# Two-layer cross-attention: layer-0 scores ahead of the value projection, and the later preparation spread over the first four units

## The chip, the cores and the metric

The kernel runs on one core of a Trainium2 chip. The metric is the device time of one execution in microseconds (us). TensorE (PE in the profile) multiplies matrices, VectorE is DVE, ScalarE is ACT, GpSimd is POOL, and SyncE is SP, which here only issues transfers. Each engine works through its own instructions in the order in which they are written, and semaphores hold an engine back until another engine or a transfer has got far enough.

## The reference

Two cross-attention layers over the same short context. x is 2 x 2048 x 512, the context is 2 x 77 x 512, the mask lets all or none of the 77 keys of a query through.

```python
# layer 0: one head of width 512
q = x @ Wq.T + bq;  k = ctx @ Wk.T + bk;  v = ctx @ Wv.T + bv
s = where(mask == 0, -1e9, q @ k.T)
x1 = softmax(s) @ v + x
# layer 1: 16 heads of width 32, then an output projection and a layer norm
Q, K, V = x1 @ Wq1.T + bq1, ctx @ Wk1.T + bk1, ctx @ Wv1.T + bv1
c = softmax(Q_h @ K_h.T / sqrt(32)) @ V_h        # for each head h
y = c @ Wo.T + bo + x1
out = layernorm(y) * gamma + beta
```

## The kernel before

The 4096 rows of x are cut into 8 blocks of 512 rows, which alternate between the two batches, and each block into 4 units; a unit is 4 heads of layer 1 (128 channels). Unit k belongs to block k // 4 and g = k % 4. Every engine runs `step(i, k)` for k = 0 to 33, which interleaves unit k with what is left of unit k - 1, the query of unit k + 1, the output projection and norm of the block before, and layer 0 of the block behind. The order inside a step is written out by hand.

Layer 0 is folded: the keys are multiplied into the query weights (`a0`, `c0`), so that scores come straight from x (`layer0`), and for each batch b the values are multiplied into layer 1's query weights (`fold`, whose product is `u`). Layer 1's query is then 14 matmuls (`query(i, k, first, last)`): 8 of x with the high and low half of the weights, 4 of x's low half, and 2 of the layer-0 probabilities with `u`. In those last two, matmuls 12 and 13, three parts of `u` are stacked on the 128 partitions: SP moves them from SBUF to SBUF with three transfers (`stack_weights`, which calls `move`, L262), and the third of these waits until VectorE has made the rest (`u_rest`). The same is done with the layer-0 probabilities of each block (`stack_probs`) and with the layer-0 value rows (`v0_a`, `v0_b`), which the output projection uses from step 5 on.

Ahead of step 0 stand the projections of the context (`project`, 32 recorded matmuls for a whole one): the keys k0T, the folded keys a0, the layer-0 values v0T, then `layer0(0, 0)`, layer 1's keys k1T, the transposes of v0T to rows (`to_rows`), `transpose0`, `fold(0)`, the first query, and between its parts layer 1's values v1T. Step 0 holds the transposes of v1T, step 1 the second fold, with `round_u(1)` on ScalarE and `u_rest(1)` on VectorE. On TensorE the wait for the second stacked `u` stands at the head of step 3, ahead of its scores:

```python
if type(i) is int and k == CH - 1:
    pe.wait_ge(u_stacked[1], 48)
...
scores(i, k)
```

Of the kernel before, what the change touches and what calls it, by code (L numbers as in the profile page):

```python
# [5 lines left out]
F32 = mybir.dt.float32  # L6
# [37 lines left out]
def xattn_kernel(nc, xT, x, mask, ctxT, w0k, w0q, w0v, w1q, w1k, w1v, w1o, cols, rows, out):  # L44
# [7 lines left out]
    with ExitStack() as ctx:  # L52
# [7 lines left out]
        with ExitStack() as prep:  # L60
            raw1 = sb("raw1", [P, CH, DIM], F32, prep)
            raw3 = sb("raw3", [P, CH, DIM], F32, prep)
            ctxT_sb = sb("ctxT_sb", [P, CH, BATCH * KEYS], F32, prep)
            v1T = sb("v1T", [P, CH, BATCH * KEYS], F32, prep)
            rest = sb("rest", [KEYS, BATCH, DIM], F32R, prep)
            v0T = sb("v0T", [P, CH, BATCH * KEYS], F32, prep)
            v0o = sb("v0o", [KEYS, BATCH, DIM], F32, prep)
            k0T = sb("k0T", [P, CH, BATCH * KEYS], F32, prep)
            raw0 = sb("raw0", [P, CH, DIM], F32, prep)
            bq0_wide = sb("bq0_wide", [P, CH, P], F32, prep)  # L70
            bo_sb = sb("bo_sb", [P, DIM], F32, prep)
            before_y = 4 * CH * BLOCK + KC * BLOCK + 2 * TILES * GCOLS
            taken = 3 * CH * DIM + 2 * BATCH * DIM + 4 * CH * BATCH * KEYS + CH * P + DIM
            sb("unused", [P, before_y - taken], F32, prep)
            raw2 = sb("raw2", [P, CH, DIM], F32, prep)
# [7 lines left out]

        wq_h = sb("wq_h", [P, CH, DIM], F32R)
# [132 lines left out]
        def _(sp):  # L217
# [5 lines left out]
            sp.dma_start(x_raw[:].rearrange("p c t -> p (c t)"), xT[0, 0]).then_inc(ld_xT, 16)  # L223
            sp.dma_start(raw3[:], w0v.rearrange("(c p) e -> p c e", p=P)).then_inc(ld_w0v, 16)
# [60 lines left out]
            stack_weights(v0_a, v0_b, slice(0, BATCH), v0_stacked, v0_h_ready, v0_ready, BATCH)  # L285

# [119 lines left out]
        def _(act):  # L406
            act.dma_start(cols_sb[:].rearrange("p a c -> p (a c)"), cols).then_inc(ld_cols, 16)
            act.dma_start(mask_sb[:].rearrange("p t k -> p (t k)"), mask[0, 0]).then_inc(ld_mask, 16)
            flat = rows.rearrange("(o n) -> o n", o=1)
            act.dma_start(bo_sb[:], flat[:, 2 * DIM:3 * DIM].to_broadcast([P, DIM])).then_inc(ld_bo, 16)  # L410
            act.dma_start(rows_sb[:].rearrange("p a d -> p (a d)"),
                          flat[:, 0:2 * DIM].to_broadcast([P, 2 * DIM])).then_inc(ld_rows, 16)
# [37 lines left out]
            leave(bank[1:3], mm_k0T, k0T, cols_sb[:, 1], k0T_ready)  # L450
            round_x(0, 0, 0, CH)
            leave(bank[5:7], mm_v0T, v0T, cols_sb[:, 2], v0T_ready)
            exp0(0, 0)
# [3 lines left out]
            act.wait_ge(bk1_ready, 1)  # L457
            leave(bank[1:3], mm_k1T, k1T, bk1_scaled, k1T_ready, scale=SCALE)
# [5 lines left out]

            round_u(0)
            leave(bank[5:7], mm_v1T, v1T, cols_sb[:, 5], v1T_ready, first=0, last=2)
            round_q(0, 0)
            leave(bank[5:7], mm_v1T, v1T, cols_sb[:, 5], v1T_ready, first=2, last=CH)
# [31 lines left out]
            def step(i, k):  # L500
                g, b = k % CH, k // CH
                round_ct(i, k - 2)
                leave_pt(i, k - 1, 0)
                exps(i, k, 0)
                if type(i) is int and k == 0:
                    for v in range(BATCH):
                        act.wait_ge(mm_v1, v + 1)
                        nc.scalar.activation(v1[:, v], bank[5 + v][0:KEYS, :], ACT.Copy).then_inc(v1_ready, 1)
                if g == 3:
                    round_p0(i, b + 1)  # L510
                leave_pt(i, k - 1, 1)
                exps(i, k, 1)
                if g == 1:
                    exps(i, k, 2)
                    round_x(i, b + 1, 0, 1)
                    exps(i, k, 3)
                    leave_pt(i, k - 1, 2)
                    round_x(i, b + 1, 1, 2)
                    leave_pt(i, k - 1, 3)
                    exp0(i, b + 1)  # L520
                else:
                    leave_pt(i, k - 1, 2)
                    exps(i, k, 2)
                    if g == 2:
# [16 lines left out]
                if type(i) is int and k == 0:  # L541
                    act.wait_ge(ld_w1o, 16)
                    for c in range(CH):
                        nc.scalar.activation(wo_h[:, c], raw3[:, c], ACT.Copy).then_inc(wo_h_ready, 1)
# [7 lines left out]
        def _(dve):  # L552
# [68 lines left out]
            dve.wait_ge(c0_ready, 1)  # L621
            layer0_leave(0, 0)
# [4 lines left out]
            for c in range(CH):  # L627
                dve.wait_ge(wq_h_ready, c + 1)
                nc.vector.tensor_tensor(wq_l[:, c], raw2[:, c], f32(wq_h[:, c]), ALU.subtract).then_inc(wq_ready, 1)
            def u_rest(b):  # L630
                dve.wait_ge(u_h_ready, b + 1)
                if b == 1:
                    dve.wait_ge(v0_stacked, 48)
                nc.vector.tensor_tensor(rest[:, b], bank[5 + 2 * b][0:KEYS, :], f32(u_a[0:KEYS, b]), ALU.subtract).then_inc(u_ready, 1)
# [3 lines left out]
            dve.wait_ge(ld_bo, 16)  # L638
            for b in range(BATCH):
                dve.wait_ge(mm_v0, b + 1)  # L640
                nc.vector.tensor_tensor(v0o[:, b], bank[3 + b][0:KEYS, :], bo_sb[0:KEYS], ALU.add).then_inc(v0o_ready, 1)
            for v in range(BATCH):
                dve.wait_ge(v0o_ready, v + 1)
                nc.vector.tensor_copy(v0_a[0:KEYS, v], v0o[:, v]).then_inc(v0_h_ready, 1)
            for v in range(BATCH):
                dve.wait_ge(v0_h_ready, v + 1)
                dve.wait_ge(u_stacked[0], 48)
# [73 lines left out]
            def step(i, k):  # L721
# [72 lines left out]
        def _(pe):  # L794
# [12 lines left out]
            def to_rows(banks, src, made):  # L807

                for b in range(BATCH):
                    for e in range(CH):  # L810
                        mm = nc.tensor.transpose(banks[b][0:KEYS, e * P:(e + 1) * P],
                                                 src[:, e, b * KEYS:(b + 1) * KEYS], ident[:])
                    mm.then_inc(made, 1)
# [142 lines left out]
            project(bank[5:7], raw3, ctxT_sb, mm_v0T, [ld_w0v, ld_w0v])  # L956
# [16 lines left out]

            transpose0(0, 0)
            fold(0, 0, CH)
            pe.wait_ge(wq_ready, CH)
            query(0, 0, 0, 3 * CH)
            pe.wait_ge(u_ready, 1)
            pe.wait_ge(p0l_ready, 1)
            project(bank[5:7], raw1, ctxT_sb, mm_v1T, [ld_w1v, ld_w1v], 0, 2)  # L980
            pe.wait_ge(u_stacked[0], 48)
            query(0, 0, 3 * CH, QUERY)
            project(bank[5:7], raw1, ctxT_sb, mm_v1T, [ld_w1v, ld_w1v], 2, CH)
            pe.wait_ge(k1T_ready, CH)
            pe.wait_ge(v0o_ready, BATCH)

            def step(i, k):
# [13 lines left out]
                if type(i) is int and k == 0:  # L1001
                    pe.wait_ge(v1T_ready, CH)
                    to_rows(bank[5:7], v1T, mm_v1)
                if type(i) is int and k == 1:
                    pe.wait_ge(v1_ready, BATCH)
# [10 lines left out]
                if type(i) is int and k == 1:  # L1016
                    pe.wait_ge(add0_done, 2)
                    fold(1, 0, 2)
                if g == 0:
# [13 lines left out]
                if type(i) is int and k == 1:  # L1033
                    fold(1, 2, CH)
                if g == 0:
# [48 lines left out]
```

## Time and profile before

| | us |
|---|---|
| median of 3 runs | 436.24 |
| lowest and highest run | 433.89, 436.6 |
| the profiled execution: its own time | 433.85 |
| its span, first to last instruction | 432.1 |
| TensorE busy | 395.1 (91%) |
| ScalarE, VectorE, GpSimd busy | 281.4, 273.3, 222.0 |

How to read it: the profile's page gives each engine's busy share in 40 slices of the span, and the chain of waits that ended last. The timeline gives groups of instructions in order of time, with the idle time before a group and what ended it. A row of windows gives busy time of each engine in one stretch, with the granted clock of TensorE in it (1.00 is 2.4 GHz, 0.50 is 1.2 GHz). The rows that the prediction uses stand in a section below.

### The profile page before, as it was taken

What the parts mean: (1) busy time and instruction counts of PE and PEld (TensorE: products, weight loads), DVE (VectorE), ACT (ScalarE), POOL (GpSimd) and SP (SyncE); (2) the same over time, 40 slices, a digit from 0 to 9 for tenths busy, and PEclk for the clock granted to TensorE, in tenths of its full rate; (3) what the DMA queues carried; (4) which work ended last, traced back from release to release, by engine and by line L of the source; (5) the groups of instructions that cost most, each with busy time, mean ns of one, the idle gap of its engine ahead of it and who ended that gap; (6) DMA issues with size and microseconds to landing.
All of it is one profiled execution on the core that took longest, in us unless ns stands there. A gap on an engine that the chain in (4) does not pass through costs nothing.

```text
span 432.1 us, 12183 instructions
## 1 busy us (share of the span) xinstructions
PE 395.1 (91%) x4968; PEld 298.2 (69%) x4968; DVE 273.3 (63%) x679; ACT 281.4 (65%) x813; POOL 222.0 (51%) x245
## 2 busy tenths in 40 slices
PE   4999997799999999999999999999999998997960
PEld 4996755577767687777777776767776776775840
DVE  0145466467766875786668776677677866476256
ACT  0432777676688676876588558856785778667122
POOL 0400366225547843784378547755576537534353
PEclk9999999999999999999999999999999999999895
DMA  8993103400042302330053005320413012600112
GB/s 263 400 324 101 41 4 126 139 6 3 2 141 77 123 2 85 133 124 2 26 189 104 24 2 168 102 72 2 165 68 110 0 31 76 215 5 9 42 49 97
DMA packets 19230, 39.44 MB, mean 91 GB/s; under 512 B 1865, under 2 KB 5449, under 8 KB 18151
## 3 DMA queue, kind: packets, MB, share of 16 engines
q1 hardware_dynamic: 18599, 37.72, 25.8%
q10 hardware_dynamic: 576, 0.96, 0.7%
q8 instruction: 39, 0.64, 0.7%
q14 instruction: 16, 0.13, 0.1%
HBM read 26.49 MB, written 8.39 MB: 81 GB/s over the span
## 4 chain that ended last, share of the span: by engine, by line
PE 75%; DVE 12%; ACT 5%; DMA 4%; issue 1%; SPq 1%; POOL 0%; DVEq 0%
PE ps_q L864 19%; PE ps_out L929 17%; PE ps_t L889 11%; PE ps_s L878 7%; PE ps_pv L904 7%; PE ps_out L825 4%; PE ps_s L801 4%; PE ps_s L944 2%; ACT prob L475 2%; DVE mx L655 2%; DMA p_b<-p_l 2%; DVE m L573 2%; DVE sm L662 1%; ACT pt L484 1%; DMA raw<-in_w0k 1%
## 5 line engine op out<-in xcount | busy, mean ns | idle before, releaser
L339 POOL TENSOR_TENSOR prob<-prob,rc 128x308 f32<-128x308 f32 x128 | 91.9, 725 | 158.8 <-DVE rc L664 157.6
L475 ACT ACTIVATE prob<-ps_s,mx 128x77 f32<-128x77 f32 x512 | 121.2, 328 | 0.7 <-DVE mx L655 0.7
L484 ACT ACTIVATE pt<-ps_t 77x512 f32<-77x512 f32 x128 | 76.3, 596 | 57.6 <-PE ps_t L889 57.0
L655 DVE TENSOR_REDUCE mx<-ps_s 128x4 f32<-128x308 f32 x128 | 54.8, 471 | 46.8 <-PE ps_s L878 46.8
L889 PE MATMUL ps_t<-ident,prob 128*77 128x128 f32 x512 | 79.8, 279 | 3.9 <-ACT pt L484 3.3
L662 DVE TENSOR_REDUCE sm<-prob 128x4 f32<-128x308 f32 x128 | 59.6, 466 | 35.0 <-ACT prob L475 34.9
L889 PEld LDWEIGHTS ps_t<-ident,prob 128*77 128x77 f32 x512 | 61.8, 148 | 23.7 <-issue 8.7
L864 PE MATMUL ps_q<-x_h,wq_h 128*128 128x512 f32 x128 | 53.4, 417 | 0.0
L864 PE MATMUL ps_q<-x_h,wq_l 128*128 128x512 f32 x128 | 53.0, 414 | 0.0
L318 POOL TENSOR_TENSOR x_l<-x_raw,x_h 128x512 fp32r<-128x512 f32 x32 | 41.2, 1292 | 21.2 <-ACT x_h L428 21.2
L929 PE MATMUL ps_out<-wo_h,ct_h 128*128 128x512 f32 x112 | 46.3, 413 | 0.0
L878 PEld LDWEIGHTS ps_s<-k1T,q 32*64 32x64 f32 x2048 | 25.8, 130 | 28.6 <-issue 15.5
L929 PE MATMUL ps_out<-wo_l,ct_h 128*128 128x512 f32 x112 | 44.3, 395 | 0.0
L929 PE MATMUL ps_out<-wo_h,ct_l 128*128 128x512 f32 x112 | 44.1, 394 | 0.0
L355 POOL TENSOR_TENSOR y<-y,rows_sb 128x512 f32<-128x512 f32 x28 | 36.0, 1286 | 13.6 <-ACT y L497 13.6
L864 PE MATMUL ps_q<-x_l,wq_h 128*128 128x512 f32 x128 | 41.0, 404 | 0.0
L357 POOL TENSOR_TENSOR y<-y,rows_sb 128x512 f32<-128x512 f32 x28 | 36.1, 1288 | 2.2
L904 PE MATMUL ps_pv<-pt,v 77*32 77x512 f32 x256 | 34.1, 602 | 1.6 <-ACT pt L484 1.6
L490 ACT ACTIVATE ct_h<-ps_pv 128x512 fp32r<-128x512 f32 x32 | 19.2, 600 | 24.8 <-PE ps_pv L904 24.7
L446 ACT ACTIVATE q<-ps_q,cols_sb 128x512 f32<-128x512 f32 x32 | 22.2, 694 | 18.2 <-PE ps_q L864 18.1
L878 PE MATMUL ps_s<-k1T,q 32*64 32x77 f32 x2048 | 31.1, 238 | 2.7 <-ACT q L446 1.8
L670 DVE TENSOR_TENSOR ct_l<-ps_pv,ct_h 128x512 fp32r<-128x512 f32 x32 | 21.8, 680 | 9.8 <-ACT ct_h L490 9.8
(111 smaller groups left out, 608.5 us busy)
## 6 DMA issues: line engine op xcount, KB each, us to landing
x_raw<-in_xT SPq DMA_DIRECT2D x8, 1024.0 KB, 6.5
y<-in_x SPq DMA_DIRECT2D x28, 256.0 KB, 2.8
out<-y SPq DMA_DIRECT2D x28, 256.0 KB, 2.0
p_b<-p_a SPq DMA_DIRECT2D x8, 154.0 KB
mask_sb<-in_mask SPq DMA_DIRECT2D x7, 154.0 KB, 5.4
raw<-in_w0k SPq DMA_DIRECT2D x2, 512.0 KB, 6.8
raw<-in_w0q SPq DMA_DIRECT2D x2, 512.0 KB, 10.0
raw<-in_w0v SPq DMA_DIRECT2D x1, 1024.0 KB, 12.2
```

The costliest lines, as they stand in the source:

```text
L318: nc.gpsimd.tensor_tensor(x_l[:, b % 2, c], x_raw[:, c], f32(x_h[:, b % 2, c]), ALU.subtract).then_inc(xl_ready, 1)
L339: nc.gpsimd.tensor_tensor(ap, ap, wide(rc[:, k % 2, h], KEYS), ALU.mult).then_inc(prob_done, 1)
L357: nc.gpsimd.tensor_tensor(y[:, t], y[:, t], rows_sb[:, 1], ALU.add).then_inc(beta_done, 1)
L475: e = nc.scalar.activation(prob[:, k % 2, h, t], ps_s[:, h, t * KEYS:(t + 1) * KEYS], ACT.Exp, bias=mx[:, k % 2, h, t:t + 1])
L484: nc.scalar.activation(pt[:, h], ps_t[0:KEYS, :], ACT.Copy).then_inc(pt_ready, 1)
L655: nc.vector.reduce_max(mx[:, k % 2, h], ps_s[:, h, 0:TILES * KEYS].rearrange("p (t k) -> p t k", k=KEYS), AX_X, negate=True).then_inc(max_ ...
L662: nc.vector.reduce_sum(sm[:, k % 2, h], prob[:, k % 2, h], AX_X).then_inc(sum_done, 1)
L864: mm = nc.tensor.matmul(ps_q[:], w, v, start=(m == 0), stop=(m == QUERY - 1))
L878: mm = nc.tensor.matmul(ps_s[r:r + P // 2, h, t * KEYS:(t + 1) * KEYS], q[rows_of, k % 2, t * P + r:t * P + r + P // 2], k1T[rows_of, g, b ...
L889: mm = nc.tensor.transpose(ps_t[0:KEYS, t * P:(t + 1) * P], prob[:, k % 2, h, t], ident[:])
L904: mm = nc.tensor.matmul(ps_pv[rows_of, :], v1[:, b % 2, own], pt[:, h], start=True, stop=True)
L929: mm = nc.tensor.matmul(ps_out[:], w, v, start=(m == 0), stop=(m == OUTPUT - 1))
```

## The change

- TensorE: `layer0(0, 0)` comes right behind the folded keys, ahead of v0T. Six matmuls of the first query come ahead of `transpose0` and `fold(0)`, the other six of its first twelve behind. k1T comes behind these. v1T moves into step 0, behind the scores, and its transposes to the end of step 0. `fold(1)` moves from step 1 to step 2. The transposes of v0T move into step 3, one batch in the middle and one near the end, and use the bank `ps_out`.
- ScalarE and VectorE follow this order: `round_u(1)` and `u_rest(1)` move to step 2, the value rows (`v0_leave`, `v0_rest`) to step 3 on VectorE; the low half of the query weights (`wq_rest`) is made around the first layer-0 softmax.
- Transfers: the first mask goes from ScalarE's queue to SP's, behind x. The two loads of bo, gamma and beta are issued by ScalarE behind its copies of k0T and not at its start. On SP the stacking of the value rows goes behind that of the second block's probabilities, and `next_inputs(0, 1)` goes ahead of these.
- `rest` and `bo_sb` get memory of their own. The wait at the head of step 3 is as it was.

```diff
@@ SP
             sp.dma_start(x_raw[:].rearrange("p c t -> p (c t)"), xT[0, 0]).then_inc(ld_xT, 16)
+            sp.dma_start(mask_sb[:].rearrange("p t k -> p (t k)"), mask[0, 0]).then_inc(ld_mask, 16)
             sp.dma_start(raw3[:], w0v.rearrange("(c p) e -> p c e", p=P)).then_inc(ld_w0v, 16)
...
             stack_weights(u_a, u_b, slice(0, 1), u_stacked[0], u_h_ready, u_ready, 1)
-            stack_weights(v0_a, v0_b, slice(0, BATCH), v0_stacked, v0_h_ready, v0_ready, BATCH)
-
             stack_weights(u_a, u_b, slice(1, 2), u_stacked[1], u_h_ready, u_ready, 2)
             sp.wait_ge(mm_u, BATCH)
             sp.wait_ge(wq_ready, CH)
             for t in range(TILES):
                 load_rows(0, 0, t)
+            next_inputs(0, 1)
             stack_probs(0, 1)
-            next_inputs(0, 1)
+            stack_weights(v0_a, v0_b, slice(0, BATCH), v0_stacked, v0_h_ready, v0_ready, BATCH)
@@ ScalarE
-            leave(bank[5:7], mm_v0T, v0T, cols_sb[:, 2], v0T_ready)
-            exp0(0, 0)
             act.wait_ge(ld_w1q, 16)
             for c in range(CH):
                 nc.scalar.activation(wq_h[:, c], raw2[:, c], ACT.Copy).then_inc(wq_h_ready, 1)
-            act.wait_ge(bk1_ready, 1)
-            leave(bank[1:3], mm_k1T, k1T, bk1_scaled, k1T_ready, scale=SCALE)
+            leave(bank[5:7], mm_v0T, v0T, cols_sb[:, 2], v0T_ready, first=0, last=2)
+            exp0(0, 0)
+            leave(bank[5:7], mm_v0T, v0T, cols_sb[:, 2], v0T_ready, first=2, last=CH)
             round_p0(0, 0)
...
-                if type(i) is int and k == 1:
+                if k == 0:
+                    round_wo(0, 3)
+                if k == 2:
                     round_u(1)
                 round_q(i, k + 1)
@@ VectorE
+            wq_rest(0)
+            wq_rest(1)
             layer0_leave(0, 0)
             layer0_mask(0, 0)
             layer0_select(0, 0)
             layer0_shift(0, 0)
+            wq_rest(2)
             layer0_probs(0, 0)
+            wq_rest(3)
...
+                if k == 3:
+                    v0_leave(0)
                 inverse_sums(i, k, 3)
-                if type(i) is int and k == 1:
+                if k == 2:
                     u_rest(1)
+                if k == 3:
+                    v0_leave(1)
+                    v0_rest(0)
+                    v0_rest(1)
@@ TensorE
-            project(bank[5:7], raw3, ctxT_sb, mm_v0T, [ld_w0v, ld_w0v])
             pe.wait_ge(a0_ready, 2)
             pe.wait_ge(c0_ready, 1)
             layer0(0, 0)
-            project(bank[1:3], raw0, ctxT_sb, mm_k1T, [ld_w1k, ld_w1k])
-            pe.wait_ge(v0T_ready, CH)
-            pe.wait_ge(ident_ready, 1)
-            to_rows(bank[3:5], v0T, mm_v0)
-            pe.wait_ge(ld_w1q, 16)
+            project(bank[5:7], raw3, ctxT_sb, mm_v0T, [ld_w0v, ld_w0v])
...
+            pe.wait_ge(wq_ready, 3)
+            query(0, 0, 0, 6)
+            pe.wait_ge(ident_ready, 1)
+            pe.wait_ge(v0T_ready, CH)
             transpose0(0, 0)
             fold(0, 0, CH)
             pe.wait_ge(wq_ready, CH)
...
```

TensorE ahead of the first unit, before (a is the folded keys, raw a weight matrix as loaded, m the layer-0 probabilities):

```order
L801 MATMUL ps_s<-k0T,raw 128x154 x16
L954 MATMUL ps_out<-k0T,bq_wide 128x154 x4
L801 MATMUL ps_t<-ctxT_sb,raw 128x154 x8
L801 MATMUL ps_pv<-ctxT_sb,raw 128x154 x8
L825 MATMUL ps_out<-a,x_raw 32x77 x64
L801 MATMUL ps_s<-ctxT_sb,raw 128x154 x16
L811 MATMUL ps_s<-ident,v0T 77x128 x8
L838 MATMUL ps_pv<-ident,m 77x128 x4
L969 MATMUL ps_t<-raw,v0T 77x512 x4
```

The same place in the change (L840 waits for a0 and c0, which VectorE copies out; the first L879 for three of the four pieces of the weights' low half; L853 for the layer-0 probabilities and v0T):

```order
L969 MATMUL ps_out<-k0T,bq_wide 128x154 x4
L840 MATMUL ps_out<-a,x_raw 32x77 x64
L818 MATMUL ps_t<-ctxT_sb,raw 128x154 x8
L818 MATMUL ps_pv<-ctxT_sb,raw 128x154 x8
L879 MATMUL ps_q<-x_h,wq_h 128x512
L879 MATMUL ps_q<-x_h,wq_l 128x512
...
L853 MATMUL ps_pv<-ident,m 77x128 x4
L979 MATMUL ps_t<-raw,v0T 77x512 x4
```

The layer-0 scores (L840) now follow the folded keys without the v0T projection between them, and the start of the first query (six matmuls of L879, of which the first is shown) stands behind v0T and ahead of the transposes.

TensorE from the end of step 2 to the transposes of step 3, in the change (L893 are the scores of step 3, which wait for q, for the exponentials of step 2 and for the second stacked `u`):

```order
L979 MATMUL ps_out<-raw,v0T 77x512 x2
L879 MATMUL ps_q<-x_l,wq_h 128x512 x2
L879 MATMUL ps_q<-p_a,u_a 128x512
L879 MATMUL ps_q<-p_b,u_b 128x512
L919 MATMUL ps_pv<-pt,v 32x512 x4
L893 MATMUL ps_s<-k1T,q 64x77 x32
L904 MATMUL ps_t<-ident,prob 77x128 x4
L853 MATMUL ps_pv<-ident,m 77x128 x4
```

The second half of the second fold (L979) now stands in the same step as, and some eight matmuls ahead of, the scores that wait for its stacked copy; before, a whole step lay between them.

SP in the change, from the second stacked `u` on (its first row waits for `round_u(1)`, its third for `u_rest(1)`):

```order
L263 DMA u_a<-u_a 51x512
L263 DMA u_b<-u_a 26x512
L263 DMA u_b<-rest 77x512
L248 DMA y<-in_x 128x512 x4
L241 DMA x_raw<-in_xT 128x2048
L242 DMA mask_sb<-in_mask 128x308
L263 DMA p_b<-p_a 77x512
L263 DMA p_a<-p_l 51x512
L263 DMA p_b<-p_l 26x512
L263 DMA v_a<-v_a 51x1024
```

Before, the x_raw and mask loads stood behind the three p moves, and the v moves ahead of the second u moves.

## Rows read from the trace of the kernel before

**Rows 1.** The page: busy shares and granted clock in 40 slices.
```profile
PE   4999997799999999999999999999999998997960
PEclk9999999999999999999999999999999999999895
```

**Rows 2.** Windows: us, busy us (count) by engine, granted clock, DMA share, GB/s.
```profile
51.59:64.46 12.87, 10.98 (x119) 6.42 (x121) 7.58 (x21) 9.45 (x28) 8.21 (x9) 1.00 0.01 2
64.46:73.47 9.01, 7.32 (x103) 5.12 (x103) 5.88 (x15) 7.94 (x25) 6.14 (x7) 1.00 0.49 153
73.47:84.56 11.09, 8.20 (x114) 5.54 (x117) 5.43 (x14) 7.41 (x23) 4.34 (x6) 1.00 0.39 114
200.00:400.00 200.00, 193.58 (x2409) 143.21 (x2408) 140.02 (x357) 146.54 (x430) 117.88 (x130) 1.00 0.23 75
```

**Rows 3.** Chain of waits ahead of step 2: start us, us, what held it.
```profile
1.24 5.00 DMA raw<-in_w0k
6.37 7.35 PE ps_s L801 x32
14.46 4.47 PE ps_s L801 x32
24.18 2.27 PE ps_out L825 x128
30.86 0.87 PE ps_s L811 x8
32.17 3.45 PE ps_t L969 x8
42.03 2.10 PE ps_pv L801 x16
46.04 3.27 PE ps_q L864 x14
```

**Rows 4.** Windows of the start: to the first matmul, and to 12.3 us.
```profile
0.00:6.20 6.20, 0.00 (x0) 0.00 (x0) 0.51 (x2) 0.00 (x0) 0.75 (x7) 1.00 0.70 193
6.37:12.30 5.93, 5.93 (x23) 5.93 (x24) 0.00 (x0) 1.39 (x2) 0.00 (x0) 1.00 1.05 371
```

**Rows 5.** Transfers: issues, KB each, us from issue to landing.
```profile
raw<-in_w1q SPq DMA_DIRECT2D x1, 1024.0 KB, 13.7
```

**Rows 6.** Timeline of SP: start us, us to issue.
```profile
7.33 2.19 SPq L225 DMA_DIRECT2D raw<-in_w1q  x1
```

**Rows 7.** Timeline of ScalarE and VectorE ahead of step 0.
```profile
29.83 2.17 ACT L456 ACTIVATE wq_h<-raw 128x512 fp32r<-128x512 f32 x4
20.02 0.32 DVE L620 COPY c<-ps_out 128x154 f32<-128x154 f32 x1 [0.57 <-PE ps_out L954]
26.60 0.48 DVE L560 TENSOR_TENSOR m<-ps_out,c 128x308 f32<-128x308 f32 x1 [6.26 <-PE ps_out L825]
28.95 0.48 DVE L592 TENSOR_TENSOR m<-m,stat 128x308 f32<-128x308 f32 x1
31.07 2.49 DVE L629 TENSOR_TENSOR wq_l<-raw,wq_h 128x512 fp32r<-128x512 f32 x4
42.07 0.69 ACT L446 ACTIVATE q<-ps_q,cols_sb 128x512 f32<-128x512 f32 x1 [0.86 <-PE ps_q L864]
```

**Rows 8.** Chain: from the first u to its stacked copy, and the probabilities' last move.
```profile
35.64 0.60 ACT u_a L463
37.83 3.42 DMA u_b<-rest
78.97 3.82 DMA p_b<-p_l
```

**Rows 9.** Timeline of TensorE: two waits, in brackets the idle time and its releaser.
```profile
41.30 0.50 PE L864 MATMUL ps_q<-p_a,u_a 128*128 128x512 f32 x1 [0.80 <-DMA u_b<-rest]
73.47 0.94 PE L878 MATMUL ps_s<-k1T,q 32*64 32x77 f32 x64 [0.83 <-ACT q L446]
```

**Rows 10.** Windows: the stretch ahead of a half clock, and the half clock.
```profile
398.00:401.40 3.40, 1.67 (x9) 1.25 (x8) 3.26 (x8) 0.86 (x2) 3.32 (x5) 1.00 0.21 80
401.40:404.80 3.40, 3.40 (x12) 2.75 (x11) 1.26 (x2) 0.24 (x1) 1.79 (x2) 0.50 0.20 77
```

More of the change, by code:

```diff
@@ L81, in xattn_kernel @@
         y = sb("y", [P, TILES, DIM])
+        rest = sb("rest", [KEYS, BATCH, DIM], F32R)
+        bo_sb = sb("bo_sb", [P, DIM])
         wq_h = sb("wq_h", [P, CH, DIM], F32R)
@@ L450, in _ @@
             leave(bank[1:3], mm_k0T, k0T, cols_sb[:, 1], k0T_ready)
+            flat = rows.rearrange("(o n) -> o n", o=1)
+            act.dma_start(bo_sb[:], flat[:, 2 * DIM:3 * DIM].to_broadcast([P, DIM])).then_inc(ld_bo, 16)
+            act.dma_start(rows_sb[:].rearrange("p a d -> p (a d)"),
+                          flat[:, 0:2 * DIM].to_broadcast([P, 2 * DIM])).then_inc(ld_rows, 16)
             round_x(0, 0, 0, CH)
-            leave(bank[5:7], mm_v0T, v0T, cols_sb[:, 2], v0T_ready)
-            exp0(0, 0)
             act.wait_ge(ld_w1q, 16)
@@ L463, in round_u, with round_wo @@
                 nc.scalar.activation(u_a[0:KEYS, b], bank[5 + 2 * b][0:KEYS, :], ACT.Copy).then_inc(u_h_ready, 1)
+            def round_wo(first, last):
+                act.wait_ge(ld_w1o, 16)
+                for c in range(first, last):
+                    nc.scalar.activation(wo_h[:, c], raw3[:, c], ACT.Copy).then_inc(wo_h_ready, 1)
             round_u(0)
-            leave(bank[5:7], mm_v1T, v1T, cols_sb[:, 5], v1T_ready, first=0, last=2)
+            act.wait_ge(bk1_ready, 1)
+            leave(bank[1:3], mm_k1T, k1T, bk1_scaled, k1T_ready, scale=SCALE)
             round_q(0, 0)
-            leave(bank[5:7], mm_v1T, v1T, cols_sb[:, 5], v1T_ready, first=2, last=CH)
             def exps(i, k, h):
@@ L504, in step @@
                 exps(i, k, 0)
[L505 to L508, printed above, removed]
                 if g == 3:
@@ L521, in step @@
                 else:
+                    if k == 0:
+                        leave(bank[5:7], mm_v1T, v1T, cols_sb[:, 5], v1T_ready, first=0, last=2)
                     leave_pt(i, k - 1, 2)
                     exps(i, k, 2)
+                    if k == 0:
+                        leave(bank[5:7], mm_v1T, v1T, cols_sb[:, 5], v1T_ready, first=2, last=CH)
                     if g == 2:
@@ L540, in step @@
                     normalise(i, b - 2, 3)
[L541 to L544, printed above, removed]
+                if k == 0:
+                    for v in range(BATCH):
+                        act.wait_ge(mm_v1, v + 1)
+                        nc.scalar.activation(v1[:, v], bank[5 + v][0:KEYS, :], ACT.Copy).then_inc(v1_ready, 1)
+                    round_wo(3, CH)
             run(act, step)
@@ L621, in _, with wq_rest @@
             dve.wait_ge(c0_ready, 1)
+            def wq_rest(c):
+                dve.wait_ge(wq_h_ready, c + 1)
+                nc.vector.tensor_tensor(wq_l[:, c], raw2[:, c], f32(wq_h[:, c]), ALU.subtract).then_inc(wq_ready, 1)
+            wq_rest(0)
+            wq_rest(1)
             layer0_leave(0, 0)
@@ L637, in _, with v0_leave, v0_rest @@
             u_rest(0)
[L638 to L642, printed above, removed]
+            def v0_leave(v):
+                dve.wait_ge(ld_bo, 16)
+                dve.wait_ge(mm_v0, v + 1)
+                nc.vector.tensor_tensor(v0o[:, v], ps_out[0:KEYS, :], bo_sb[0:KEYS], ALU.add).then_inc(v0o_ready, 1)
                 dve.wait_ge(v0o_ready, v + 1)
                 nc.vector.tensor_copy(v0_a[0:KEYS, v], v0o[:, v]).then_inc(v0_h_ready, 1)
-            for v in range(BATCH):
+            def v0_rest(v):
                 dve.wait_ge(v0_h_ready, v + 1)
-                dve.wait_ge(u_stacked[0], 48)
+                dve.wait_ge(u_stacked[v], 48)
                 nc.vector.tensor_tensor(rest[:, v], v0o[:, v], f32(v0_a[0:KEYS, v]), ALU.subtract).then_inc(v0_ready, 1)
@@ L805, in project, with to_rows @@
                         mm.then_inc(made, 1)
[L807 to L813, printed above, removed]
+            def to_rows(to, src, b, made):
+                for e in range(CH):
+                    mm = nc.tensor.transpose(to[0:KEYS, e * P:(e + 1) * P], src[:, e, b * KEYS:(b + 1) * KEYS], ident[:])
+                mm.then_inc(made, 1)
             def layer0(i, b):
@@ L976, in _ @@
             pe.wait_ge(wq_ready, CH)
[L977 to L980, printed above, removed]
+            query(0, 0, 6, 3 * CH)
+            project(bank[1:3], raw0, ctxT_sb, mm_k1T, [ld_w1k, ld_w1k])
             pe.wait_ge(u_stacked[0], 48)
             query(0, 0, 3 * CH, QUERY)
-            project(bank[5:7], raw1, ctxT_sb, mm_v1T, [ld_w1v, ld_w1v], 2, CH)
             pe.wait_ge(k1T_ready, CH)
-            pe.wait_ge(v0o_ready, BATCH)
             def step(i, k):
@@ L1000, in step @@
                 scores(i, k)
[L1001 to L1004, printed above, removed]
+                if k == 0:
+                    pe.wait_ge(u_ready, 1)
+                    pe.wait_ge(p0l_ready, 1)
+                    project(bank[5:7], raw1, ctxT_sb, mm_v1T, [ld_w1v, ld_w1v])
+                if k == 1:
                     pe.wait_ge(v1_ready, BATCH)
@@ L1015, in step @@
                     last_output(0, 3, [1])
-                if type(i) is int and k == 1:
+                if k == 2:
                     pe.wait_ge(add0_done, 2)
                     fold(1, 0, 2)
+                if k == 3:
+                    pe.wait_ge(u_ready, 2)
+                    to_rows(ps_out, v0T, 0, mm_v0)
                 if g == 0:
@@ L1032, in step @@
                 transposes(i, k - 1, 3)
-                if type(i) is int and k == 1:
+                if k == 0:
+                    pe.wait_ge(v1T_ready, CH)
+                    for v in range(BATCH):
+                        to_rows(bank[5 + v], v1T, v, mm_v1)
+                if k == 2:
                     fold(1, 2, CH)
+                if k == 3:
+                    pe.wait_ge(v0o_ready, 1)
+                    to_rows(ps_out, v0T, 1, mm_v0)
                 if g == 0:
```

19 lines of the change are left out of this document (4 added, 15 removed).

## The prediction

> **What bounds the kernel now.** I read the page first. TensorE is busy in nearly every slice, and its granted clock is full until close to the end [rows 1]. The reader is to see that the matrix work sets the time: of the 200 us in the middle it fills 193.58 [rows 2]. The change leaves out no matmul and adds none; it only puts them in another order, all of it ahead of step 4. So it can win only idle time of TensorE in the first 85 us, and whatever it wins or loses there is kept to the end, since the steps behind have hardly any slack to give back.
>
> Then I took windows of the steps. Step 1 lasts 12.87 us with 10.98 busy, step 2 9.01 with 7.32, step 3 11.09 with 8.20 [rows 2]: 1.9, 1.7 and 2.9 us idle. Ahead of step 0 TensorE waits 5.00 us for the first half of w0k, and 0.80 us for the stacked u [rows 3, 9]. That, 6.5 us in the steps, and the 0.76 us from the end of the first projection (6.37 + 7.35 us) to 14.46 is all that there is to win [rows 3]. Last I read the timelines and the chain for the lengths of single pieces.
>
> **The start.** Until 6.2 us the transfers moved 193 GB/s times 6.2 us, 1.2 MB [rows 4]. The first matmul needs the context (0.32 MB by its size) and half of w0k (0.52 MB). The other 0.36 MB are mask, bo, gamma and beta, which ScalarE's queue issued alongside; at the 371 GB/s of the next stretch they are worth 1.0 us. They now go later. I take **-1.0 us**; between nothing (the queue of SP is no faster alone) and -1.4. The first matmuls run slowly: 23 in 5.93 us until 12.3 us, then 11 of the same kind in the 1.4 us that are left, about the two levels of the clock, although the column says 1.00 for the first stretch [rows 3, 4]. I let that slow stretch keep its length.
>
> **From there to step 0**, on a clock that starts 1.0 us earlier. The folded keys a0 run from 13.4 to 17.9 (4.47 us), c0 to 18.9. Layer-0 scores now come at once, and must wait for VectorE's copy of c0, which before started at 20.02, 0.04 after its matmul, and took 0.32 [rows 7]: a new wait of 0.4 us, which v0T covered before. Scores end at 21.6 (2.27), v0T at 25.8 (twice 2.10) [rows 3]. The first query needs three pieces of the low half of the weights. w1q landed at 7.33 + 13.7 = 21.0 us [rows 5, 6], and I leave it there, since the same bytes stand ahead of it. ScalarE rounds a piece in 0.54 (2.17 for four), so two are there at 22.1, and VectorE's two subtractions (0.62 each) end at 22.9. Only then does VectorE start on the layer-0 scores, which lay ready at 21.6. Its chain to the shifted scores took from 26.60 to 29.43 [rows 7], 2.8 us; it ends at 25.8 and the third piece at 26.4. TensorE waits 0.6 us. Six query matmuls (3.27 us for 14) give 27.8, transposes 28.3, fold 31.8 (3.45), six more 33.2, k1T 37.6. The first u took from 35.64 to 37.83 + 3.42 = 41.25 to be stacked [rows 8], 5.6 us; from 31.8 that is 37.4, just hidden by k1T. With k1T gone from there it would be 4.2 us of waiting, so this cover is thin. Two matmuls and ScalarE's 0.69 us for q then lie open [rows 7], 0.8 us, because v1T no longer stands over them: step 0 starts at 39.2. New waits 0.4 + 0.6 + 0.8, one of 0.8 gone: **+1.0 us**, between 0 (w1q lands earlier, since less competes with it early) and +2 (the stacked u behind the loads of w1o and x, which SP now issues later).
>
> **Step 0** takes in v1T and its transposes. ScalarE's copies of it stand between exponentials and are done before the query ends. Cover: v1T's 4.2 us and the query's 3.3; without it each copy (0.7 us for two) would show. Nothing.
>
> **Step 1** loses the fold (3.45). Its two halves stood over ScalarE's exponentials and copies of the transposes, so part of what goes comes back as idle time: I take 2.6 us instead of 1.9, **+0.7**, between 0 and +1.7 (half of the fold).
>
> **Step 2** gains the fold, and there it fills the 1.7 us of idle time whole: 7.32 + 3.45 = 10.8 us without a gap. **-1.7**, at the least -1.2. The wait for q at the end of it, 0.83 us [rows 9], is part of that.
>
> **Step 3: the wait that was free.** The scores of step 3 stand behind the wait for the second stacked u, which only matmuls 12 and 13 of the next query need. Before, u came out of step 1 and was in place long ahead. Now the fold ends some eight matmuls (4 of the query, 4 of the context, 0.23 us each, 1.9 us) before TensorE gets to these scores: 8.9 us into a step of 10.8. ScalarE takes u behind its last exponentials and a rounding of x, at about 9.1, and 5.6 us later it is stacked, at 14.7. TensorE stands still from 10.8 on: **+4.0 us**. Behind that wait are queued the scores, with them VectorE's maxima, ScalarE's exponentials, GpSimd's scaling, and the layer-0 transposes; nothing runs meanwhile that TensorE will need less of. At the least 3.0 (u taken at once, a shorter landing), at the most 5.0 (ScalarE half a us late, y's loads in the way). The row has 3.42 us from issue to landing of the last part. The Trainium skill, "DMA: Bandwidth & Descriptors", section "Anatomy of one DMA — SWDGE (gpsimd) path", gives a fixed 2.0 us plus the bytes at 436 GB/s, so 2.4 us for this one: by that the wait is 3.0 and the sum 1.0 smaller; the row is of this very transfer, and decides.
>
> **The rest of step 3.** The value rows' transposes (0.87 us in all [rows 3]) come in. The first half fills a wait for the copies; the second must wait until VectorE has taken the first out of `ps_out`, an operation as long as a wq_l (0.62), and delays the last query matmuls by some 0.5 us. Work +0.9, length +0.6: **-0.3**, between -0.6 and +0.3. SP moves p behind the loads of y and x now, 2 MB, but these are issued at the end of the wait and the p moves 5 us later: hidden; if they were not, half a us. Removing v0's moves from ahead of u's costs nothing, SP stood idle.
>
> **The clock.** After a stretch with 1.67 busy of 3.40 us TensorE got half clock for 3.40 us, near the end [rows 10]. In the wait of 4.0 us it does nothing at all. I expect the same there: 3.4 us at half clock are worth up to 1.7 us, but half of step 3's start waits for other engines: **+0.8**, between 0 and 1.7.
>
> Sum: -1.0 + 1.0 + 0.7 - 1.7 + 4.0 - 0.3 + 0.8 = **+3.5 us**. Against the profiled execution's own 433.85 us (its span of 432.1 and 1.75 around it) that is 437.35. That execution was at the low end of the runs; against their median of 436.24 it is 439.7, and that is my number.
>
> **Rivals.**
> 1. *Slower than 1%.* The clock stays at half for a second such stretch, so that the wait costs 3.4 us of clock and not 0.8: +6.1, 442.3. For it: no stretch in [rows 10] is as idle as this wait. Against: the half clock there lasted one stretch although TensorE was only just back at work. It decides once more than 1.7 us are lost. The change not doing at the start what it says (w0k no earlier, +4.5, 440.7) leads near it too. Together 0.30.
> 2. *The clock is kinder.* No half clock at the wait (-0.8), the slow first stretch shorter (5.93 us at half clock cost 3.0; half as long, -1.5), the one near the end missing (-1.7): 3.5 - 4.0 = -0.5, 435.7. For it: all three hang on where the clock changes. Against: the end of the program is untouched. 0.14. The Trainium skill, "TensorE: Matmul & The Clock Gate", section "What's actually happening", says that activity releases the throttle and idleness brings it back, and that the point of change shifts from run to run: it bears on both cases.
> 3. *Faster than 1%.* The stacked u is in place before the scores of step 3, so the wait costs nothing, and the clock is as in 2: -4.5, 431.7. It would need 5.6 us of stacking in 1.7. 0.06.
>
> The forecast itself, 437.3 to 440.6, has 0.50. The bounds of the terms, taken as independent, give 2.3 us to either side of the sum, 437.4 to 442.0; with case 2 and the second stretch of case 1 the range is 435.5 to 442.5. About 1% (4.4 us) can be told from no change. Faster by over that: 0.06; slower: 0.30; between: 0.64.
>
> **What would show it.** Right: TensorE idle for about 4 us ahead of the scores of step 3, released by the transfer of u's rest; the first matmul near 5.3 us; step 0 starting near 39, step 3 near 75 and step 4 near 87 where it was 84.56; step 2 without gaps; a 0.50 in the clock at 75. Wrong: a wait under 3 us or none there; step 0 later than 41 (the front then lost what it won); step 1 shorter than 9.5. The total is wrong if steps 4 to 33 differ in length between the two, where I expect none.

## The result, and the profile after

| | before | after |
|---|---|---|
| median (4 runs each) | 435.06 | 444.81 |
| lowest and highest | 433.89, 436.6 | 439.73, 448.04 |
| profiled execution, own time | 433.85 | 439.73 |
| its span | 432.1 | 437.9 |

The ratio is 1.0197, 95% interval 1.014 to 1.0253: slower, by 1.4 to 2.5%. Run again on another occasion the changed kernel took 443.36 us against 433.91 (ratio 1.0191, 1.0134 to 1.0248). The ratios leave out every execution more than 1.5% above the fastest of its kernel, such as the 448.04 here, while the medians count all. The sum for the profiled execution, 437.35, missed its 439.73 by 2.4 us, and it is the fastest of the four; the median lies 5 us above it.

The page after. TensorE's busy time is the same 395.1 us; the clock row has its dent at slice 8, where before there was none [rows 1]:

```profile
PE   4888977889999999999999999999999998999860
PEclk9999999699999999999999999999999999999995
```

The wait that was forecast, in the timeline of TensorE after (start us, us, work, and in brackets the idle time before it and its releaser). Step 3's scores start at 77.89, 4.14 us after TensorE had reached them:

```profile
63.20 0.95 PE L893 MATMUL ps_s<-k1T,q 32*64 32x77 f32 x64
...
72.68 1.06 PE L919 MATMUL ps_pv<-pt,v 77*32 77x512 f32 x8
...
77.89 1.42 PE L893 MATMUL ps_s<-k1T,q 32*64 32x77 f32 x64 [4.14 <-DMA u_b<-rest]
...
88.99 0.66 PE L827 MATMUL ps_out<-ident,v0T 128*77 128x128 f32 x4 [1.25 <-DVE v0o L652]
...
91.51 1.01 PE L893 MATMUL ps_s<-k1T,q 32*64 32x77 f32 x64
```

Windows after: steps 1, 2 and 3 (to compare with [rows 2]), then the wait and what follows it (start and end, us, then busy us and in brackets the count of instructions for PE, PEld, DVE, ACT and POOL, then the granted clock, the DMA share and GB/s):

```profile
52.27:63.20 10.93, 7.62 (x108) 5.09 (x103) 7.34 (x21) 7.72 (x24) 5.39 (x6) 1.00 0.00 1
63.20:73.75 10.55, 10.54 (x114) 6.35 (x110) 5.85 (x15) 8.42 (x25) 8.45 (x10) 1.00 0.01 2
77.89:91.51 13.62, 11.45 (x114) 8.39 (x114) 7.85 (x19) 7.01 (x22) 2.80 (x4) 0.76 0.50 178
73.75:77.40 3.65, 0.00 (x0) 0.00 (x0) 0.00 (x0) 0.60 (x1) 0.79 (x1) 1.00 0.41 107
77.50:84.30 6.80, 5.83 (x79) 4.76 (x80) 3.48 (x8) 2.03 (x6) 0.22 (x1) 0.50 0.89 326
```

Step 2 has no gap, as forecast. In the wait TensorE is busy for 0.00 us, and from 77.5, shortly before it ends, the clock is at 0.50 for 6.8 us, twice as long as in [rows 10].

And the front, timeline of TensorE: behind the first wait for w0k five gaps up to the scores of step 0, 3.7 us together, where before there was one of 0.80, beside the 0.76 for k0T that both kernels have [rows 9] (two of the five have no releaser in the profile, marked issue; the first of them, 0.46, stands where the wait for c0 was forecast):

```profile
5.53 6.23 PE L818 MATMUL ps_s<-ctxT_sb,raw 128*128 128x154 f32 x32 [5.53 <-DMA raw<-in_w0k]
...
18.50 2.35 PE L840 MATMUL ps_out<-a,x_raw 128*32 128x77 f32 x128 [0.46 <-issue]
...
24.55 1.58 PE L818 MATMUL ps_pv<-ctxT_sb,raw 128*128 128x154 f32 x10 [0.62 <-issue]
...
26.81 0.50 PE L879 MATMUL ps_q<-x_h,wq_h 128*128 128x512 f32 x1 [0.68 <-DVE wq_l L630]
...
38.99 0.50 PE L879 MATMUL ps_q<-p_a,u_a 128*128 128x512 f32 x1 [1.05 <-DMA u_b<-rest]
...
40.59 0.94 PE L893 MATMUL ps_s<-k1T,q 32*64 32x77 f32 x64 [0.87 <-ACT q L441]
```

### The profile page after: what moved, and what is told of

Read it like the earlier page. It is cut to its first block, busy times and chain, and to the rows that moved or that the text cites. A ratio compares the mean times of both kernels' runs of the same rounds, so it can differ in the third digit from the quotient of the medians.

```text
span 437.9 us, 12183 instructions
## 1 busy us (share of the span) xinstructions
PE 395.1 (90%) x4968; PEld 297.9 (68%) x4968; DVE 272.0 (62%) x679; ACT 281.3 (64%) x813; POOL 221.7 (51%) x245
## 4 chain that ended last, share of the span: by engine, by line
PE 72%; DVE 12%; DMA 6%; ACT 5%; SPq 2%; issue 2%; POOL 0%; DVEq 0%
PE ps_q L879 20%; PE ps_out L944 17%; PE ps_t L904 11%; PE ps_s L893 7%; PE ps_pv L919 6%; PE ps_out L840 4%; DMA raw<-in_w1q 3%; ACT prob L478 2%; PE ps_s L959 2%; DMA u_b<-rest 2%; DVE mx L666 2%; ACT pt L487 2%; DVE m L579 1%; DVE sm L673 1%; PE ps_pv L853 1%
## 5 line engine op out<-in xcount | busy, mean ns | idle before, releaser
L879 PE MATMUL ps_q<-x_h,wq_h 128*128 128x512 f32 x128 | 54.4, 425 | 0.7 <-DVE wq_l L630 0.7
L879 PE MATMUL ps_q<-x_h,wq_l 128*128 128x512 f32 x128 | 53.6, 419 | 0.0
L893 PEld LDWEIGHTS ps_s<-k1T,q 32*64 32x64 f32 x2048 | 26.1, 133 | 32.2 <-issue 15.1
L355 POOL TENSOR_TENSOR y<-y,rows_sb 128x512 f32<-128x512 f32 x28 | 36.0, 1286 | 12.1 <-ACT y L500 12.1
L879 PE MATMUL ps_q<-x_l,wq_h 128*128 128x512 f32 x128 | 41.0, 404 | 0.0
L893 PE MATMUL ps_s<-k1T,q 32*64 32x77 f32 x2048 | 31.3, 241 | 6.3 <-DMA u_b<-rest 4.1
L493 ACT ACTIVATE ct_h<-ps_pv 128x512 fp32r<-128x512 f32 x32 | 19.1, 598 | 26.2 <-PE ps_pv L919 26.2
L879 PEld LDWEIGHTS ps_q<-x_h,wq_h 128*128 128x128 f32 x128 | 24.7, 193 | 4.1 <-DVE wq_l L630 0.9
```

Source lines behind the costliest of these rows:

```text
L355: nc.gpsimd.tensor_tensor(y[:, t], y[:, t], rows_sb[:, 0], ALU.mult).then_inc(gamma_done, 1)
L879: mm = nc.tensor.matmul(ps_q[:], w, v, start=(m == 0), stop=(m == QUERY - 1))
L893: mm = nc.tensor.matmul(ps_s[r:r + P // 2, h, t * KEYS:(t + 1) * KEYS], q[rows_of, k % 2, t * P + r:t * P + r + P // 2], k1T[rows_of, g, b ...
```

## The experiments

Ratios are to the kernel before in runs on the same chips, with their 95% intervals.

| kernel | median us | ratio |
|---|---|---|
| changed, again | 443.36 | 1.0191 (1.0134 to 1.0248) |
| changed, late wait | 446.48 | 1.0274 (1.023 to 1.0318) |
| before + second fold in step 2 | 439.01 | 1.0116 (1.0074 to 1.0157) |
| changed, wait filled | 440.60 | 1.0146 (1.0098 to 1.0195) |
| changed, p ahead of loads | 444.80 | 1.0220 (1.0163 to 1.0278) |
| both of these | 439.03 | 1.0069 (1.0032 to 1.0107) |
| and the first u ahead of loads | 433.69 | 0.9987 (0.9955 to 1.0019) |
| and VectorE's order | 433.91 | 0.9976 (0.994 to 1.0012) |
| before + the loads alone | 433.97 | 0.9981 (0.9958 to 1.0005) |
| changed, fold back in step 1 | 438.27 | 1.0086 (1.0056 to 1.0116) |
| VectorE's order + split fold | 436.32 | 1.0050 (1.002 to 1.008) |
| and the second rows late | 434.31 | 0.9989 (0.9961 to 1.0016) |

**The changed kernel again.** 

> The changed kernel once more, unaltered, for the spread of its runs and a second profile. Theory W (the wait ahead of the scores of step 3 and the half clock that follows it): the wait is again 4.0 to 4.3 us, and only the length of the half clock behind it differs from execution to execution; the median is 441 to 446, over 5 us above before. Rival F (the new order ahead of step 0 is what varies): the wait is the same and step 0 starts later than 41 us in a slower execution.

Its profiled execution (442.02 us) waited 3.93 us ahead of step 3 and was at half clock from 77.8 to 84.6 us, much as the first; it started step 4 within 0.1 us of it. It took 2.2 us longer behind step 4 and shows one more half-clock stretch near the end. Theory W had the wait to within 0.1 us and the median right, but what differed between these two was the end, not the half clock behind the wait, and step 0 started at 41.0 at the latest (40.59 and 40.97).

**The wait moved to its reader.**

```diff
-                if type(i) is int and k == CH - 1:
-                    pe.wait_ge(u_stacked[1], 48)
...
                             wait(pe, p0_stacked, 48 * (blocks(i, b) + 1))
+                            if b == 1:
+                                pe.wait_ge(u_stacked[1], 48)
```

> The changed kernel with the wait for the second stacked u put right ahead of the two query matmuls that read it. Theory W: no idle time ahead of the scores of step 3, no half clock near 77 us, so 4.1 us of wait and all of the clock loss are gone; but the probabilities' moves now stand behind the loads of y and x on the same queue and land 1 to 2 us late: median 434 to 436.5, about as before. Rival F (front): 440 or more, since the front is untouched. Rival V (the value rows inside step 3 cost more than thought): 438 to 440.

A miss of 10 us: 446.48, slower than the changed kernel. The wait ahead of step 3 is gone, and in its place stand two others. Timeline of SP, and the chain of waits (start us, us):

```profile
79.98 1.86 SPq L248 DMA_DIRECT2D y<-in_x  x4
81.94 0.38 SPq L241 DMA_DIRECT2D x_raw<-in_xT  x1
...
84.46 0.80 SPq L263 DMA_DIRECT2D p_b<-p_l  x1
```

```profile
34.60 5.86 DMA u_b<-rest
...
84.46 7.57 DMA p_b<-p_l
```

The last probability move landed 7.57 us after its issue, with 2 MB of y and x issued 2.1 to 4.5 us ahead of it; in [rows 8] it took 3.82. TensorE waited 3.50 us for it and fell to half clock from 89.3 to 99.6. And the first u, behind the loads of w1o and x, landed after 5.86 us: TensorE waited 2.53, and was at half clock from 41.5 to 48.4. The first of these two the wait at step 3 had hidden: in the changed kernel's trace p's moves are issued 4.8 to 6.4 us behind the load of x. The second is not from this edit: the code is the changed kernel's up to there.

**One part alone: the second fold in step 2, in the kernel before.**

```diff
-                if type(i) is int and k == 1:
+                if type(i) is int and k == 2:
                     pe.wait_ge(add0_done, 2)
                     fold(1, 0, 2)
```

(and the same for its second half, `round_u(1)` and `u_rest(1)`)

> The kernel before, with one part of the change alone: the second fold, its rounding and its rest in step 2 and not in step 1, the wait at the head of step 3 as it was. Theory W: step 1 shorter by about 2.7 us, step 2 longer by about 1.7, then 4 us of wait and a half clock behind it: 439 to 446, slower than before by 4 us or more. Rival F: within 1 us of before, 434 to 436.5.

Theory W holds: 439.01, ratio 1.0116. Its timeline has the wait, as long as in the changed kernel, and half clock from 75.9 to 82.7. Step 1 became shorter by 1.2 us only, not by 2.7 (from 12.87 to 11.64):

```profile
77.09 1.42 PE L878 MATMUL ps_s<-k1T,q 32*64 32x77 f32 x64 [4.21 <-DMA u_b<-rest]
```

**The same delay without the idleness.**

```diff
                 if type(i) is int and k == CH - 1:
+                    for m in range(17):
+                        nc.tensor.matmul(ps_t[:], wq_h[:, m % CH, 0:P], x_h[:, 0, m % CH], start=True, stop=True)
                     pe.wait_ge(u_stacked[1], 48)
```

> The changed kernel with 17 extra matmuls of 512 columns ahead of the wait at the head of step 3 (they write a free bank, nobody reads the result), so that TensorE works for the 4.0 us in which it stood still. The delay is the same, only the idleness is gone. Theory W with the clock as the larger half: no half clock behind the wait, 437 to 439, and runs within 1 us of each other. Rival (the clock costs little, the loss beyond the wait is elsewhere): 442 to 446 as the changed kernel, with its spread.

440.60: between the two ranges. The clock did what the theory said, the time and its spread did not. In its profiled execution step 3 starts at 77.68, as late as in the changed kernel, but at full clock, and takes 11.60 us, not 13.62:

```profile
77.68:89.28 11.60, 8.97 (x116) 6.42 (x115) 7.84 (x19) 7.03 (x22) 2.80 (x4) 1.00 0.58 195
```

So the half clock there costs 2.0 us, beside 4.1 of plain waiting. The runs still spread over 7 us, so something else varies from execution to execution.

**The probability moves ahead of the loads, the wait as it was; then both.**

```diff
+            stack_probs(0, 1)
+            next_inputs(0, 1)
             sp.wait_ge(mm_u, BATCH)
             sp.wait_ge(wq_ready, CH)
             for t in range(TILES):
                 load_rows(0, 0, t)
-            next_inputs(0, 1)
-            stack_probs(0, 1)
```

> The changed kernel with the second block's probability moves put ahead of the loads of y and x on SP, the wait at the head of step 3 left as it was. If the wait hides the queue's order (theory W2), nothing moves: 4.1 us of wait, half clock behind it, 441 to 446. Rival (the order on the queue costs on its own, also in the changed kernel): 2 to 4 us less than the changed kernel, 438 to 441.

> Both together: the wait for the second u ahead of the two matmuls that read it, and the probability moves ahead of the loads. Theory W2 (wait and queue order each hide the other's cost; both must go): the probabilities land within 4 us of their last move and not 7.6, step 4 starts near 85.5 where that of the changed kernel starts at 91.6, 434 to 437. Rival (the first u, behind the loads of w1o and x, with a half clock behind it, is what makes it slow): 438 to 442.

Alone the order on SP changes nothing that can be told (444.80); with the late wait it is 439.03, 7.4 us below the late wait alone (2.0% by the ratios). Each hid the other's cost. No wait for p is left ahead of step 4, but step 4 starts at 89.0 us and not near 85.5, since step 1 already starts at 56.0. The kernel stays 0.7% above before: theory W2 was too low by 2 us, and the rival's place, the first u, is where the next experiment puts the rest. The chain of waits of this kernel:

```profile
33.94 6.38 DMA u_b<-rest
...
90.22 8.63 DMA v_b<-rest
```

The value rows' last move shows the same behind y and x, and costs 0.57 us at step 5.

**The first block's moves ahead of the loads too.**

```diff
-            sp.wait_ge(mm_v0T, 2)
-            sp.dma_start(raw3[:], w1o.rearrange("(c p) e -> p c e", p=P)).then_inc(ld_w1o, 16)
...
-            next_inputs(0, 0)
             stack_probs(0, 0)
             stack_weights(u_a, u_b, slice(0, 1), u_stacked[0], u_h_ready, u_ready, 1)
+            next_inputs(0, 0)
+            sp.wait_ge(mm_v0T, 2)
+            sp.dma_start(raw3[:], w1o.rearrange("(c p) e -> p c e", p=P)).then_inc(ld_w1o, 16)
```

> As the one before, and the moves of the first block's probabilities and of the first u also ahead of the loads of x and w1o. The first u lands 3.1 to 3.4 us after its last move (4.4 to 5.9 with the loads ahead), TensorE waits under 0.3 us for it, and there is no half clock near 41 us: 432.5 to 435, 1 to 2.5 us below the one before and with less spread. Rival (its landing depends on the move alone): no difference.

433.69: 5.3 us less in the median (0.8% by the ratios), and the kernel is level with before. TensorE goes from k1T into matmul 12 without a wait, and there is no half clock between the first slow stretch and 366.9 us:

```profile
35.83 2.39 PE L818 MATMUL ps_s<-ctxT_sb,raw 128*128 128x154 f32 x17
37.96 0.50 PE L881 MATMUL ps_q<-p_a,u_a 128*128 128x512 f32 x1
```

The bytes on the way when the moves of u began (last number: GB/s). They were issued from 36.3 us on before, from 33.0 in the changed kernel and from 33.3 in this one, and the windows are 34 to 38 us of before and 30 to 34 of the other two:

```profile
34.00:38.00 4.00, 4.00 (x15) 2.55 (x14) 2.04 (x4) 0.59 (x1) 0.00 (x0) 1.00 0.25 76
```

```profile
30.00:34.00 4.00, 4.00 (x16) 2.33 (x15) 0.94 (x2) 0.60 (x1) 0.00 (x0) 1.00 1.01 394
```

```profile
30.00:34.00 4.00, 4.00 (x15) 2.08 (x14) 1.22 (x2) 0.60 (x1) 0.00 (x0) 1.00 0.24 73
```

Here x and w1o are issued 0.9 and 1.8 us behind u's last move, on the same queue, and it had landed 3.1 us after its issue at the latest (34.85 to 37.96). The ten traces in which the load of x goes first show what its landing hangs on: it came 12.1 to 13.6 us after x was issued in all of them. With the last move issued 9.3 us behind x it took 3.10 to 3.42 us, 8.3 us behind 3.81, 7.9 to 8.0 us behind 4.38 and 4.86, and 7.0 to 7.4 us behind 5.56 to 6.38. No run puts the loads on another queue, so whether the order on the queue or the loads' traffic as such delays the move is not shown.

**VectorE takes the layer-0 scores first.**

```diff
-            wq_rest(0)
-            wq_rest(1)
             layer0_leave(0, 0)
             layer0_mask(0, 0)
             layer0_select(0, 0)
             layer0_shift(0, 0)
+            wq_rest(0)
+            wq_rest(1)
             wq_rest(2)
```

> As the one before, and VectorE takes the layer-0 scores, ready at about 21 us, ahead of the low half of the query weights, ready from 22 us. The three pieces that the first query waits for come at 25.6 and not 26.8: 0.6 to 0.9 us less, 432 to 434.5. Rival (the query then waits as long for something else): the same as the one before.

433.91, not to be told from the one before; the rival had it. The wait for the weights' third piece is gone from its timeline (1.46 us in the one before), but its projections started 0.4 us later, and 0.86 us without a releaser stand in v0T.

**The two loads alone, in the kernel before.**

```diff
-            act.dma_start(mask_sb[:].rearrange("p t k -> p (t k)"), mask[0, 0]).then_inc(ld_mask, 16)
             flat = rows.rearrange("(o n) -> o n", o=1)
...
             leave(bank[1:3], mm_k0T, k0T, cols_sb[:, 1], k0T_ready)
+            act.dma_start(bo_sb[:], flat[:, 2 * DIM:3 * DIM].to_broadcast([P, DIM])).then_inc(ld_bo, 16)
```

(gamma and beta with bo; the mask on SP behind x)

> The kernel before with one part of the change alone: the loads of bo, gamma and beta behind the copies of k0T, and the mask on SP's queue behind x. If these loads took bandwidth from w0k, its first matmul starts near 5.5 us and not 6.0 to 6.4, and the time is 0.5 to 1.5 us below before. Rival (TensorE's work in the front is held by something else, and the later loads come in the way of w1q): within 0.5 us of before.

433.97, ratio 0.9981 (0.9958 to 1.0005): at best 0.4%. In the profiled execution the first matmul came at 6.50 us, no earlier than in [rows 3]; but in the eleven profiled executions with the changed kernel's loads and front it came at 5.33 to 6.24, in the two with the loads as before at 5.93 and 6.37. The forecast 1.0 us is neither shown nor excluded.

**The second fold back in step 1, all else changed.**

```diff
-                if k == 2:
+                if k == 1:
                     pe.wait_ge(add0_done, 2)
                     fold(1, 0, 2)
```

> The changed kernel with the second fold, its rounding and rest back in step 1, all else as changed. Theory W2: no wait ahead of the scores of step 3, so 4.1 us and the half clock behind it are gone; step 2 has its 1.7 us of idle time again; the load of x still stands ahead of the probabilities on SP (1 us or more of wait for them at the end of step 3), and the first u still lands behind the loads of w1o and x: 436 to 440. Rival (the wait was not the main loss): 442 to 446.

438.27. Against the changed kernel's 1.0191 that is 1.05%, some 4.6 us, for the fold's place; put alone into the kernel before it cost 1.16%. The two agree. It is less than the 4.1 of waiting and 2.0 of clock, since the fold fills idle time in step 2. What is left, 0.86%, is within the intervals that of both order edits together (0.69%), and its trace has the first u 5.56 us after its last move, with half clock from 41.3 to 48.1.

**Half of the fold in step 1.**

```diff
+                if k == 1:
+                    pe.wait_ge(add0_done, 2)
+                    fold(1, 0, 2)
                 transposes(i, k - 1, 3)
...
                 if k == 2:
-                    pe.wait_ge(add0_done, 2)
-                    fold(1, 0, 2)
+                    fold(1, 2, CH)
```

(and v's moves ahead of y's loads)

> The version with late wait, both probability moves and the first u ahead of the loads, and VectorE's new order, and now half of the second fold in step 1, ahead of its last transposes, half in step 2; the moves of the value rows also ahead of the loads of y. The first half fills the 1.7 us wait that step 1 has there, so that step 2 is shorter by 1.7 and the sum by about 1.5; no wait for the value rows at step 5 (0.6 to 0.7 us): 431 to 433. Rival (step 1 is bound by ScalarE, and the half fold lengthens it as much): 433.5 to 435.

> As the one before, and the transposes of the second value rows in step 3 stand behind two more of the query's matmuls. They wait 1.24 us for VectorE now; two matmuls of 0.23 us each come out of that wait: 0.4 us less, hardly to be told from the one before. Rival: the same, or longer by the time in which the last matmuls wait for the probabilities instead.

The half fold fills the wait in step 1: the 1.74 us ahead of its last transposes are gone, and the step is no longer for it (10.93 us; 11.19 in the one before). But TensorE now gets to the end of step 2 1.27 us early and waits there for q, so step 2 is 0.2 us shorter and not 1.7 (10.27 for 10.49). The 1.05 us for ct_l, which were there before, follow, and the clock falls to half where it had not; step 3 takes 13.16 us for 11.60:

```profile
72.36 0.95 PE L895 MATMUL ps_s<-k1T,q 32*64 32x77 f32 x64 [1.27 <-ACT q L441]
...
74.96 1.10 PE L853 MATMUL ps_pv<-ident,m 128*77 128x128 f32 x4 [1.05 <-DVE ct_l L681]
```

436.32: both were wrong. The gain that was forecast is taken back by the wait for q and the clock, and step 1 was not lengthened, as the rival had it. With the second rows late it is 434.31; their wait went from 1.25 to 0.78 us, but the 2 us between these two medians are more than that, and the first of the two has 1.39 us without a releaser at the scores of step 5. Why the second is faster stays open. No version clearly beats the kernel before.

## Why the prediction was wrong

Its direction and its main mechanism were right; its size was not, and the median of 444.81 lies 2.3 us above the range. The profiled execution, 439.73, lies inside it.

- **Right: the wait.** +4.0 forecast, 4.14 and 3.93 measured in two executions of the changed kernel, 3.76 with p ahead of the loads, and 4.21 in the kernel before with the fold moved. Step 2 lasts 10.55 us (10.8 forecast), step 3 without half clock 11.60 (11.7). Step 1 lasts 10.93, 0.8 more than forecast (12.87 - 3.45 + 0.7 = 10.1), inside the bounds of its term.
- **The step that failed: "From there to step 0", +1.0, and in it the first stacked u, "just hidden by k1T".** In the changed kernel's profiled execution the gaps ahead of step 0 grew from 0.80 to 3.7 us, by 2.9 and not 1.0. The 5.6 us for this u were taken from a trace in which little else was on the way (76 GB/s from 34 to 38 us, 394 in the changed kernel from 30 to 34). The change issues w1o and x at 26.2 and 26.6 us and this u's moves from 33.0; before, x went out at 28.5 and the moves from 36.3. Its last move took 3.10 to 3.42 us to land in the kernel before and its two relatives, and 3.81 to 6.38 in the seven executions with the changed front. TensorE then waited 0.5 to 3.05 us, and in four of the seven the clock fell to half with it. In these four step 1 starts at 55.6 to 56.7 us, in the other three at 51.8 to 52.7; I had forecast 50.9. The bound of +2 was for the waiting alone, without the clock. Moving this u ahead of the loads took 3.6 us off (0.82%), and this with the fold's 4.6 makes 8.2 of the 8.3 us that the changed kernel is slower. The sum adds differences from different kernels as if they were independent. And both profiled executions of the changed kernel itself (waits of 1.05 and 1.53 us) kept their clock at this place; that its slower executions lose it there is concluded from its relatives with the same front.
- **The clock's term** was 0.8, at most 1.7; it cost 2.0 in step 3, since it stayed at half for 6.8 us. That is rival 1's event, at 2.0 of the 3.4 us that it was given. It was wrong to price the clock at one place only: every wait that I left thin was also a place where it could fall.
- **The start**: -1.0 for w0k came out as 0.84 in this execution (the first matmul at 5.53 and not 6.37), though the loads alone do not show it. The slow first stretch was 2.3 us shorter (to 9.2 us, not 12.3), worth another 1.1, the first projection taking 6.23 us and not 7.34. Both helped the profiled execution, against which the sum was 2.4 us off, and hid part of the front's loss.
- **Behind step 4** I expected no difference. The profiled execution of the changed kernel needs 346.4 us from there to its end, the kernel before 347.6, the other twelve from 347.4 to 351.3. The time grows with the number of half-clock stretches between 360 and 418 us: none in 346.4 and 347.4, one in 347.6 to 349.9, two in 349.2 to 351.3. Why there are more in one execution than in another no run here shows.
- "Hidden; if they were not, half a us" on p behind y and x: hidden, as long as the wait stood. Uncovered, it was 3.5 us of waiting and 10 us at half clock.
- **Slips in its working.** The terms for step 0 as written reach 38.9 us and not 39.2. Steps 3 and 4 "near 75" and "near 87" do not fit its own sum, which gives 75.8 and 88.1; measured were 77.89 and 91.51.

The Trainium skill's rule that was weighed ("DMA: Bandwidth & Descriptors", section "Anatomy of one DMA — SWDGE (gpsimd) path", by estimate 2.4 us for such a move) was too low for every one of these landings; the shortest was 3.05. The same page's section "Queues, rings and completion order" says that on each engine descriptors are consumed in ring order; the traces fit this, with 3.1 us for the first u's last move when it is issued 9.3 us behind the load of x, and 7.57 to 8.76 for the moves of p and v with 2 MB issued just ahead.

## What to carry to other kernels

In this kernel the landing of a small move from SBUF to SBUF that TensorE waits for changed with the loads issued ahead of it, from 3.1 to 8.8 us. When an order is rewritten, put such moves ahead of bulk loads, and price the landing from a row that has the same loads ahead of it. A wait should stand at its reader, but before it is moved there, look for what it hides: here its removal alone made the kernel slower. And a wait on TensorE can cost more than its length: count for each one the half clock that may follow, and be careful with filling one gap if that makes another.

## What the runs showed of the hardware

- TensorE's clock fell to half (0.50, 1.2 GHz) within 1.3 us of the end of a wait of 2.24 to 3.05 us at the first u in four executions, and stayed there for 3.4 or 6.8 us; after waits of 0.48, 1.05 and 1.53 us at the same place it did not. It fell after pairs of shorter waits as well: 1.27 and 1.05 us in both versions with the split fold, 0.83 and 1.05 us in the kernel before with the loads moved; after this same pair the kernel before and the changed kernel with the fold back in step 1 kept their clock.
- The same wait of 4 us, filled with 17 matmuls whose result nobody reads, left the clock full in the profiled execution and made the next step 2.0 us shorter there.
- The last move of the first u landed 12.1 to 13.6 us after the load of x was issued in ten executions, whether it was itself issued 7.0 or 9.3 us behind that load.
- The slow stretch at the start ended between 8.5 and 12.3 us, with the first matmul at 5.3 to 6.5. In it a matmul of 128x154 was recorded with 462 to 466 ns, behind it with 292 to 298, while the column of the granted clock says 1.00 for both.
